# Channel attention taps read from PSUM, and five steps of a transformer pipeline in another order

## The chip, the cores and the metric

The kernel runs on one core of a Trainium2 chip. The metric is the device time of one execution in microseconds, the median of several runs. Engines are TensorE (PE; its weight loads are PEld), VectorE (DVE), ScalarE (ACT), GpSimd (POOL) and SyncE (SP, which issues all DMAs).

## The reference

A hybrid network over 16 images of 96 channels and 16x16 pixels, in four parts. Cut to what matters:

```python
x = x + conv_attention(group_norm(x))    # channel attention, 8 heads: q, k, v of 1x1 and depthwise 3x3 taps
x = large_conv_block(x)                  # 1x1, depthwise 13x13, gelu
t = tokens(x)                            # 16 x 256 tokens of 96
t = t + attention_2(ln(t))               # 6 heads over 512 tokens, own token masked
t = t + experts_2(ln(t))                 # 4 experts, top 2, hidden 384
t = t + attention_3(ln(t))               # causal
t = t + experts_3(ln(t))

# channel attention, per image (d = 12 channels a head, n = 256 pixels)
qkv = depthwise3x3(einsum('bchw,oc->bohw', x, w_qkv))
q, k = l2norm(q), l2norm(k)
attn = softmax(einsum('bhdn,bhen->bhde', q, k) * temperature)
out = einsum('bhde,bhen->bhdn', attn, v) @ w_proj
```

## The kernel before

The engines run programs of their own and meet at semaphores; the order on each engine is written out by hand. There are three stages.

**Channel attention** (`channel_attention`, 45 to 222 us) is a pipeline over 16 images; image b is worked on in `slot` b % 2. In step b TensorE computes the products of queries and keys of image b+1 (`queries_keys`) and its values with the nine value taps (`value_taps`, laid between the other work), and, for image c = b-1, turns q and scaled k (`turn`), multiplies the scores and applies the attention (`result`). ScalarE copies the raw products of queries and keys from PSUM bank 0 or 1 to the SBUF tile `raw` (`keep`, L449). VectorE applies the nine depthwise taps to them (`convolve`): L612 writes the first one, L615 adds the other eight, for q and k in turn, each as sum <- raw x tap + sum, 18 instructions an image. Seven taps stand before `maximum` of the image before, one between it and `attention`, the last behind. For image c ScalarE squares and sums q and k (`squares`), POOL makes the inverse norms out of the two sums (`norms`: L299, L301, L303, on 96x2 numbers), and ScalarE scales k by them (`scale_k`, L464). TensorE may overwrite a bank of raw products once ScalarE has copied it (`pe.wait_ge(s_raw, b)`).

**The large convolution** (222 to 323 us) is not touched.

**The transformer** (`transformer`, 324 us on) is a software pipeline over 16 pairs of images, i, the first 8 for layer 2 and the last 8 for layer 3, in two halves u each, one image a half (n = 2i + u). In half (i, u) run: attention of image n; the rest of attention of image n-1 (`weighted_values`, `turn_heads`, `turn_out`, `project`); two of the four experts (e0, e1) of pair j = i-2. In the first half (u = 0) also queries and keys of pair i+1, in the second (u = 1) values of i+1, the input of the experts of i-1 and the transposed input of i+2.

The scores of an image come in three blocks (`scores(n, 0..2)`) from which VectorE takes maxima; these are split in three bf16 parts, turned by TensorE (`turn_maxima`, L1087), copied by ScalarE as rows beside the queries (`rows`, L1288, `tr_qs`), and the scores are computed again, transposed, with the maxima subtracted (`transposed_scores(n, 0..2)`, L1095). ScalarE takes the exponential of each block (`exponential`, L1295, to `tr_pT`), and POOL sets the masked ones to zero (`masked(n, 0)` waits for the second exponential, `masked(n, 1)` for the third; L999). The third block uses the same PSUM banks as the first, so it waits for the first exponential; the next image's first scores (L1079) wait for the third one.

Queries and keys go into the products as three bf16 parts each: ScalarE makes the first from PSUM (`first_part`) and the second from VectorE's rest (`second_part`, L1284), POOL the third (`third_parts`, L993), and SP carries them through DRAM into the stacks `qs` and `ks` of the next pair. The experts' input is split too: `xh` (`high_input`, ScalarE, L1316) and `xl` (`low_input`, POOL, L988). The first product of an expert (`hidden`, L1143) needs both. `result` (L1153) is the second product: 24 matmuls in the trace for 4 blocks of tokens and 3 of hidden. `add_experts` (VectorE, L1492) adds it to the tokens, `add_bias` (L1500) adds the bias, `gates` (13 small instructions up to L1480) computes the gate. The two preloads of ScalarE's tables (L1333, L1345) stand at fixed places of a half.

## Time and profile before

| | us |
|---|---|
| median of 3 runs | 1042.7 (1040.33 to 1043.45) |
| the profiled execution | 1046.85 |
| its span | 1045.1 |

| stretch of the span, us | length | PE | DVE | ACT | POOL | TensorE clock |
|---|---|---|---|---|---|---|
| 60 to 180, channel attention | 120 | 94.7 | 73.2 | 47.7 | 36.1 | 0.79 |
| 180 to 255, its end and the start of the convolution | 75 | 54.6 | 41.8 | 23.0 | 38.2 | 0.68 |
| 300 to 1045, nearly all transformer | 745 | 633.9 | 399.8 | 427.5 | 313.1 | 0.92 |

The clock is the share of TensorE's full speed that was granted: 1.00 is 2.4 GHz and 0.50 is 1.2 GHz, and a mean between them mixes stretches at either. A busy TensorE is not one at its peak. The idle time in square brackets is what an engine spent before an instruction, with the engine, tile and line that ended it; times of instructions that overlap in the engine's pipeline are longer than their distance from start to start.

### The profile page before, as it was taken

How to read it: one execution, taken by the hardware profiler on the slowest of the kernel's cores; microseconds unless marked ns; L12 is line 12 of the kernel's file. 1: busy time of each engine (PE TensorE's matmuls, PEld its weight loads, DVE VectorE, ACT ScalarE, POOL GpSimd, SP SyncE). 2: the span in 40 equal slices, each digit the busy share in tenths (PEclk: the TensorE clock that was granted, in tenths of full speed). 3: DMA queues.
4: the chain of work that ended last, by engine and by line, in shares of the span. 5: the costliest groups of instructions: out<-in, count | busy, mean ns of one | idle time of the engine just before them, and what ended most of it. 6: DMA issues, size and time to landing. Idle time of an engine off the chain costs nothing.

```text
span 1045.1 us, 17189 instructions
## 1 busy us (share of the span) xinstructions
PE 857.4 (82%) x6224; PEld 697.2 (67%) x6224; DVE 576.9 (55%) x1684; ACT 515.6 (49%) x809; POOL 405.8 (39%) x428
## 2 busy tenths in 40 slices
PE   2878778678984375989998898998998998998887
PEld 1655556447983254777776786787787787777776
DVE  5855666628644236566557647656656555555431
ACT  1234334340013234566566676575575575575554
POOL 3232232346004124436436345355454444444422
PEclk9987877758996568799899999999999999999899
DMA  3700000001100333032030230230230330330000
GB/s 77 118 13 0 0 0 0 1 0 18 20 1 2 67 69 68 2 68 63 7 69 24 46 69 16 55 68 11 60 69 18 68 69 14 71 69 9 9 1 16
DMA packets 29000, 37.20 MB, mean 36 GB/s; under 512 B 10696, under 2 KB 25856, under 8 KB 28928
## 3 DMA queue, kind: packets, MB, share of 16 engines
q1 hardware_dynamic: 28928, 36.24, 16.6%
q8 instruction: 45, 0.74, 0.3%
q14 instruction: 27, 0.22, 0.1%
HBM read 25.06 MB, written 11.17 MB: 35 GB/s over the span
## 4 chain that ended last, share of the span: by engine, by line
PE 40%; ACT 11%; issue 6%; DVE 5%; POOL 5%; DMA 1%; SPq 1%; POOLq 0%; DVEq 0%; ACTq 0%
PE ps L1143 11%; PE ps L1153 9%; ACT tr_pT L1295 4%; PE ps L1079 4%; PE ps L1108 3%; PE ps L1095 3%; PE ps L1064 3%; POOL tr_pT L999 2%; ACT tr_hid L1311 2%; ACT tr_qs L1288 2%; PE ps L1081 2%; ACT L1345 2%; POOL tr_xl L988 2%; DVE tr_mf L1403 2%; PE ps L1113 1%
## 5 line engine op out<-in xcount | busy, mean ns | idle before, releaser
L1311 ACT ACTIVATE tr_hid<-ps,b 128x512 f32<-128x512 f32 x192 | 131.9, 688 | 136.4 <-PE ps L1143 135.8
L1153 PE MATMUL ps<-w,tr_hid 128*128 128x96 f32 x1536 | 182.4, 275 | 4.1 <-DVE tok L1492 4.1
L1153 PEld LDWEIGHTS ps<-w,tr_hid 128*128 128x128 f32 x1536 | 177.9, 192 | 6.4 <-issue 5.0
L999 POOL TENSOR_SCALAR_AFFINE_SELECT tr_pT<-tr_pT 128x768 f32<-128x768 f32 x64 | 55.4, 866 | 308.3 <-ACT tr_pT L1295 308.3
L1403 DVE TENSOR_REDUCE tr_mf<-ps 128x4 f32<-128x1024 f32 (+2 forms) x96 | 103.7, 1088 | 81.6 <-PE ps L1081 80.9
L1295 ACT ACTIVATE tr_pT<-ps 128x1024 f32<-128x1024 f32 (+1 forms) x96 | 86.3, 917 | 82.0 <-PE ps L1095 82.0
L1492 DVE SCALAR_TENSOR_TENSOR tok<-ps,tr_gate,tok 128x96 f32<-128x96 f32 x224 | 55.6, 311 | 121.6 <-PE ps L1153 119.6
L1079 PE MATMUL ps<-keys,tr_qs 96*128 96x256 bf16 (+1 forms) x384 | 77.7, 280 | 44.0 <-ACT tr_pT L1295 29.5
L1143 PE MATMUL ps<-tr_xh,tr_wh 96*128 96x512 f32 x192 | 90.1, 469 | 20.7 <-POOL tr_xl L988 19.5
L615 DVE SCALAR_TENSOR_TENSOR ca_qk<-ca_raw,dw,ca_qk 96x225 f32<-96x225 f32 (+1 forms) x256 | 98.8, 452 | 0.0
L299 POOL TENSOR_SCALAR ca_rn<-ca_ss 96x2 f32<-96x2 f32 x16 | 39.5, 2468 | 133.5 <-ACT ca_sq L455 133.5
L1079 PEld LDWEIGHTS ps<-keys,tr_qs 96*128 96x128 bf16 x384 | 39.7, 104 | 72.5 <-issue 43.6
L363 PE MATMUL ps<-ca_xn,wT 96*96 96x240 f32 (+2 forms) x288 | 85.6, 448 | 0.0
L1143 PE MATMUL ps<-tr_xh,tr_wl 96*128 96x512 f32 x192 | 78.8, 410 | 0.0
L1143 PE MATMUL ps<-tr_xl,tr_wh 96*128 96x512 f32 x192 | 78.1, 407 | 0.0
L363 PEld LDWEIGHTS ps<-ca_xn,wT 96*96 96x96 f32 x288 | 58.9, 210 | 18.0
L1143 PEld LDWEIGHTS ps<-tr_xh,tr_wh 96*128 96x128 f32 x192 | 37.3, 194 | 39.0 <-POOL tr_xl L988 22.6
L1288 ACT COPY tr_qs<-ps 18x1536 bf16<-18x1536 bf16 x32 | 45.8, 1432 | 31.9 <-PE ps L1087 31.6
L1095 PE MATMUL ps<-tr_qs,keys 114*128 114x256 bf16 (+1 forms) x384 | 51.6, 274 | 1.5 <-ACT tr_qs L1288 0.8
L1391 DVE TENSOR_TENSOR tr_rest<-ps,tr_part 96x512 f32<-96x512 f32 x32 | 22.0, 687 | 46.9 <-ACT tr_part L1280 46.9
L713 PE MATMUL ps<-cv_cin,cv_packed 128*128 x208 | 39.7, 354 | 6.6 <-DVE cv_packed L773 4.0
L993 POOL TENSOR_TENSOR tr_part<-tr_rest,tr_part 96x512 bf16<-96x512 f32 x32 | 42.2, 1336 | 5.9 <-ACT tr_part L1284 4.0
(234 smaller groups left out, 1731.2 us busy)
## 6 DMA issues: line engine op xcount, KB each, us to landing
parts<-tr_part SPq DMA_DIRECT2D x96, 96.0 KB
tr_qs<-parts SPq DMA_DIRECT2D x16, 288.0 KB, 4.2
keys<-parts SPq DMA_DIRECT2D x16, 288.0 KB, 5.4
tr_qs<-parts SPq DMA_DIRECT2D x16, 192.0 KB, 5.7
keys<-parts SPq DMA_DIRECT2D x16, 192.0 KB, 6.3
w<-in_L_ffn_w SPq DMA_DIRECT2D x4, 576.0 KB
chan<-in_x SPq DMA_DIRECT2D x4, 384.0 KB, 5.1
windows<-lines_d SPq DMA_DIRECT2D x96, 13.0 KB, 1.6
```

The lines of the kernel that those rows point to most:

```text
L363: ins = nc.tensor.matmul(dst[:, y0:y1, x0:x1], m.wT[0:C, M_V0 + 3 * (dy + 1) + dx + 1, :], x[:, y0 + dy:y1 + dy, x0 + dx:x1 + dx], start=( ...
L615: nc.vector.scalar_tensor_tensor(dst[:, y0:y1, x0:x1], src[:, y0 + dy:y1 + dy, x0 + dx:x1 + dx], m.dw0[:, t, k:k + 1], dst[:, y0:y1, x0:x1 ...
L999: pool.affine_select(out=block, in_=block, compare_op=ALU.is_ge if causal(n // 2) else ALU.not_equal, fill=0.0, base=0, pattern=[[0, H], [ ...
L1079: nc.tensor.matmul(view[:, c, :], qs[0:C, slot, h, u, P * t:P * (t + 1)], ks[0:C, slot, h, u, 0:width], start=True, stop=False)
L1095: ins = nc.tensor.matmul(view[:, c, :], ks[:, slot, h, u, P * t:P * (t + 1)], qs[:, slot, h, u, N - width:N], start=True, stop=True)
L1143: ins = nc.tensor.matmul(ps[:, H0 + step % 2, :], w[:, e, P * c:P * (c + 1)], x[:, :], start=(n == 0), stop=(n == 2))
L1153: ins = nc.tensor.matmul(ps[:, RES, C * t:C * (t + 1)], hid[:, e % 2, c, P * t:P * (t + 1)], m.ffn[j // PAIRS].w2[:, e * HC + c, :], start ...
L1288: nc.scalar.copy(qs[C:KR, n // 2 % 2, :, n % 2, :], max_rows()).then_inc(s_mr, 1)
L1295: nc.scalar.activation(flat[:, H * t + h:H * t + h + len(units), N - width:N], slot_view(slot_bank(k), len(units), width), ACT.Exp).then_i ...
L1311: nc.scalar.activation(hid[:, e % 2, c, :], ps[:, H0 + step % 2, :], ACT.Gelu, bias=m.ffn[j // PAIRS].b1[:, step:step + 1]).then_inc(s_h, 1)
L1403: nc.vector.tensor_reduce(mf[:, n % 2, 0, H * t + h:H * t + h + len(units)], slot_view(slot_bank(k), len(units), width), AX.X, ALU.max, ne ...
L1492: ins = nc.vector.scalar_tensor_tensor(fin[:, t, :] if last else m.tok[:, tile, :], ps[:, RES, C * t:C * (t + 1)], gate[:, tile, e:e + 1], ...
```

## The change

Channel attention: `keep`, the tile `raw` and its semaphore are gone. `convolve` reads the raw products from the PSUM bank. VectorE waits for TensorE's products directly, and TensorE waits for all nine taps of image b-1, for q and for k, before it writes the bank again.

Transformer, TensorE: `result` is cut in two parts of 12 matmuls each. `turn_maxima` stands between the parts of e0, and `transposed_scores(n, 2)` between the parts of e1, ahead of `project` and `gate_products`. ScalarE: `second_part` of both images stands behind the third exponential instead of before it. POOL: `low_input` stands before `masked(n, 1)` instead of behind it. `rows` stays on ScalarE.

```diff
@@ channel attention, TensorE
-                            pe.wait_ge(s_raw, b)
+                            for t in range(2):
+                                pe.wait_ge(s_tap[t], 9 * b)
                         queries_keys(b + 1, other)
@@ channel attention, ScalarE
-                def keep(b, slot):
-                    act.wait_ge(s_qk, b + 1)
-                    nc.scalar.copy(raw[:, slot, :, :].rearrange("p t n -> p (t n)"), ps[0:C, slot, :]).then_inc(s_raw, 1)
...
-                    if ahead:
-                        if back:
-                            for t in range(2):
-                                act.wait_ge(s_tap[t], 9 * b)
-                        keep(b + 1, other)
@@ channel attention, VectorE
-                            src = raw[:, slot, t, :].rearrange("p (y x) -> p y x", x=WW)
+                            src = ps[0:C, slot, N * t:N * (t + 1)].rearrange("p (y x) -> p y x", x=WW)
...
-                    dve.wait_ge(s_raw, b + 1)
+                    dve.wait_ge(s_qk, b + 1)
@@ transformer, POOL
+                        if u == 1 and 0 <= i - 1 < LAST:
+                            low_input(i - 1)
                         if i < LAST:
                             masked(n, 1)
-                        if u == 1 and 0 <= i - 1 < LAST:
-                            low_input(i - 1)
@@ transformer, TensorE
-                def result(j, e):
-                    pe.wait_ge(s_h, 12 * j + 3 * e + 3)
-                    if j or e:
-                        pe.wait_ge(s_ac, 4 * j + e)
-                    for t in range(4):
+                def result(j, e, part):
+                    if part == 0:
+                        pe.wait_ge(s_h, 12 * j + 3 * e + 3)
+                        if j or e:
+                            pe.wait_ge(s_ac, 4 * j + e)
+                    for t in range(2 * part, 2 * part + 2):
...
+                        result(j, e0, 0)
                     if att:
                         turn_maxima(n)
...
-                        result(j, e0)
+                        result(j, e0, 1)
...
-                        result(j, e1)
+                        result(j, e1, 0)
+                    if att:
+                        pe.wait_ge(s_ex, 3 * n + 1)
+                        transposed_scores(n, 2)
+                    if ffn:
+                        result(j, e1, 1)
                     if chain:
                         project(n - 1)
...
-                    if att:
-                        pe.wait_ge(s_ex, 3 * n + 1)
-                        transposed_scores(n, 2)
@@ transformer, ScalarE
                         first_part(i + 1, 1, H1)
-                        second_part(i + 1, 0)
-                        second_part(i + 1, 1)
...
                         exponential(n, 2)
+                    if u == 0 and i + 1 < LAST:
+                        second_part(i + 1, 0)
+                        second_part(i + 1, 1)
```

The rows below are instructions in program order, with the semaphores that they wait for.

TensorE, from the turned maxima to the next scores, in a second half with expert work. First before:

```order
L1087 MATMUL ps<-ident_b,maxima 114x128 [waits at_max_parts]
L1153 MATMUL ps<-w_2,tr_hid 128x96 [waits ff_added,ff_gelu]
L1095 MATMUL ps<-tr_qs,keys 128x256 [waits at_max_rows]
L1069 MATMUL ps<-wT,tr_xT 128x96 [waits at_rest1,ff_gelu]
L1153 MATMUL ps<-w_2,tr_hid 128x96 [waits ff_added,ff_gelu]
L1153 MATMUL ps<-w_2,tr_hid 128x96 x11
L1133 MATMUL ps<-wT,outT 128x96 [waits at_outT]
L1166 MATMUL ps<-gate,tr_xTF 128x4 [waits ff_xT,at_v_kept]
L1095 MATMUL ps<-tr_qs,keys 128x256 [waits at_exp]
L1058 MATMUL ps<-ident,tr_xnA 96x128 [waits at_normed,ff_xT]
L1079 MATMUL ps<-keys,tr_qs 128x256 [waits at_exp,at_stacks0]
```

And now:

```order
L1144 MATMUL ps<-w_2,tr_hid 128x96 [waits ff_added,ff_gelu]
L1144 MATMUL ps<-w_2,tr_hid 128x96 x5
L1077 MATMUL ps<-ident_b,maxima 114x128 [waits at_max_parts]
L1144 MATMUL ps<-w_2,tr_hid 128x96 x6
L1085 MATMUL ps<-tr_qs,keys 128x256 [waits at_max_rows]
L1059 MATMUL ps<-wT,tr_xT 128x96 [waits at_rest1,ff_gelu]
L1085 MATMUL ps<-tr_qs,keys 128x256 [waits at_exp]
L1144 MATMUL ps<-w_2,tr_hid 128x96 x6
L1123 MATMUL ps<-wT,outT 128x96 [waits at_outT]
L1158 MATMUL ps<-gate,tr_xTF 128x4 [waits ff_xT,at_v_kept]
L1048 MATMUL ps<-ident,tr_xnA 96x128 [waits at_normed,ff_xT]
L1069 MATMUL ps<-keys,tr_qs 128x256 [waits at_exp,at_stacks0]
```

The turned maxima have half a result ahead of them, and the third transposed scores (the second row that reads `tr_qs,keys`) have half a result, the projection and the gate products behind them.

POOL in the same half, around the experts' low input `tr_xl` and the masks on `tr_pT`. Before:

```order
L961 TENSOR_TENSOR tr_xnA<-tr_xnA,rstd 128x384 [waits at_pool_own]
L999 AFFINE_SELECT tr_pT<-tr_pT 128x6x128 [waits at_exp] x2
L988 TENSOR_TENSOR tr_xl<-tr_xTF,tr_xh 96x512 [waits ff_x_high]
L1010 TENSOR_TENSOR tr_bias<-tr_gate,b_2 128x384 [waits ff_tok_biased,ff_gate_dve]
L1010 TENSOR_TENSOR tr_term<-tr_gate,b_2 128x384 [waits ff_bias_own]
```

And now:

```order
L951 TENSOR_TENSOR tr_xnA<-tr_xnA,rstd 128x384 [waits at_pool_own]
L989 AFFINE_SELECT tr_pT<-tr_pT 128x6x128 [waits at_exp]
L978 TENSOR_TENSOR tr_xl<-tr_xTF,tr_xh 96x512 [waits ff_x_high]
L989 AFFINE_SELECT tr_pT<-tr_pT 128x6x128 [waits at_exp]
L1000 TENSOR_TENSOR tr_bias<-tr_gate,b_2 128x384 [waits ff_tok_biased,ff_gate_dve]
```

The low input stands between the two masks. ScalarE in a first half, from the first exponential on. Before:

```order
L1295 ACTIVATE tr_pT<-ps 128x1024 [waits at_scoresT]
L1280 CAST tr_part<-ps 96x2x256 [waits at_parts_stored,at_qk]
L1284 CAST tr_part<-tr_rest 96x2x256 [waits at_rest1] x2
L1295 ACTIVATE tr_pT<-ps 128x1024 [waits at_scoresT]
L1333 ACT_TABLE_LOAD
```

And now:

```order
L1291 ACTIVATE tr_pT<-ps 128x1024 [waits at_scoresT]
L1276 CAST tr_part<-ps 96x2x256 [waits at_parts_stored,at_qk]
L1291 ACTIVATE tr_pT<-ps 128x1024 [waits at_scoresT]
L1280 CAST tr_part<-tr_rest 96x2x256 [waits at_rest1] x2
L1329 ACT_TABLE_LOAD
```

The two second parts (`tr_part<-tr_rest`) have moved behind the last exponential of the half.

## Rows read from the trace of the kernel before

**Rows 1.** Windows between maxima: length, busy PE, PEld, DVE, ACT, POOL, clock

```profile
81.09:93.11 12.02, 11.70 (x40) 8.42 (x40) 7.25 (x23) 4.77 (x15) 2.51 (x3) 0.58 0.00 0
...
117.37:128.21 10.84, 7.84 (x40) 5.71 (x40) 7.23 (x22) 4.50 (x14) 3.73 (x3) 0.95 0.00 0
...
sum 155.08, PE 119.28 PEld 88.05 DVE 94.06 ACT 60.55 POOL 46.75; mean PE 9.18 PEld 6.77 DVE 7.24 ACT 4.66 POOL 3.60
```

**Rows 2.** DVE timeline: start us, us, instruction, [idle before <-releaser]

```profile
119.61 0.60 DVE L612 TENSOR_SCALAR ca_qk<-ca_raw,dw 96x256 f32<-96x256 f32 x2
120.14 4.54 DVE L615 SCALAR_TENSOR_TENSOR ca_qk<-ca_raw,dw,ca_qk 96x225 f32<-96x225 f32 x12
128.21 0.25 DVE L621 TENSOR_REDUCE ca_nm<-ps 96x1 f32<-96x96 f32 x1 [3.54 <-PE ps L405]
```

**Rows 3.** Timelines of POOL and ScalarE around the norms, and the last image

```profile
120.67 0.42 ACT L455 ACTIVATE ca_sq<-ca_qk 96x256 f32<-96x256 f32 x1 [0.26 <-DVE ca_qk L615]
...
121.92 2.83 POOL L299 TENSOR_SCALAR ca_rn<-ca_ss 96x2 f32<-96x2 f32 x1 [8.03 <-ACT ca_sq L455]
124.84 0.71 POOL L301 TENSOR_TENSOR ca_rn<-ca_rn,power 96x2 f32<-96x2 f32 x1
...
125.84 0.51 ACT L464 ACTIVATE ca_kn<-ca_qk,ca_rn 96x256 f32<-96x256 f32 x1 [3.59 <-POOL ca_rn L303]
...
216.81 0.21 POOL L299 TENSOR_SCALAR ca_rn<-ca_ss 96x2 f32<-96x2 f32 x1 [6.88 <-ACT ca_sq L455]
217.10 0.71 POOL L301 TENSOR_TENSOR ca_rn<-ca_rn,power 96x2 f32<-96x2 f32 x1
```

**Rows 4.** Line L299: ns least/median/most, first and last start us

```profile
L299 POOL TENSOR_SCALAR ca_rn<-ca_ss x16: 214/2505/3763, 40.4 to 216.8; 96x2 f32<-96x2 f32 x16
```

**Rows 5.** L993 on POOL (ns min/median/max, starts), DVE timeline beside it

```profile
L993 POOL TENSOR_TENSOR tr_part<-tr_rest,tr_part x2: 1151/1378/1606, 608.3 to 609.8; 96x512 bf16<-96x512 f32 x2
...
608.30 0.55 DVE L1500 TENSOR_TENSOR tok<-tok,tr_bias 128x384 f32<-128x384 f32 x1
608.88 0.99 DVE L1492 SCALAR_TENSOR_TENSOR tok<-ps,tr_gate,tok 128x96 f32<-128x96 f32 x4
```

**Rows 6.** Timeline of TensorE in a step at full clock

```profile
126.40 0.38 PE L395 MATMUL ps<-ident,ca_qk 96*128 96x96 f32 x2 [2.67 <-ACT ca_kn L464]
...
132.09 1.76 PE L363 MATMUL ps<-ca_xn,wT 96*96 96x256 f32 x8
137.25 0.58 PE L395 MATMUL ps<-ident,ca_qk 96*128 96x96 f32 x2 [3.40 <-ACT ca_kn L464]
```

**Rows 7.** Windows of 2 us, columns as in Rows 1

```profile
100.00:102.00 2.00, 0.00 (x0) 0.00 (x0) 0.41 (x2) 0.42 (x2) 1.38 (x3) 0.84 0.00 0
102.00:104.00 2.00, 1.86 (x7) 1.55 (x8) 0.00 (x0) 1.48 (x4) 0.00 (x0) 0.50 0.00 0
```

**Rows 8.** TensorE waits from 300 us on: us in total, times, longest

```profile
PE ps L1079 <- ACT tr_pT L1295: 29.5, 31, 3.1
PE ps L1143 <- POOL tr_xl L988: 19.5, 15, 3.1
PE ps L1087 <- DVE maxima L1417: 16.7, 12, 5.6
```

**Rows 9.** Timelines of ScalarE, TensorE, VectorE in one pair of halves

```profile
588.23 1.02 ACT L1295 ACTIVATE tr_pT<-ps 128x1024 f32<-128x1024 f32 x1 [3.26 <-PE ps L1095]
...
591.46 0.50 PE L1143 MATMUL ps<-tr_xh,tr_wh 96*128 96x512 f32 x1 [1.23 <-POOL tr_xl L988]
...
594.29 2.36 DVE L1403 TENSOR_REDUCE tr_mf<-ps 128x4 f32<-128x1024 f32 x2
...
595.98 0.28 PE L1079 MATMUL ps<-keys,tr_qs 96*128 96x256 bf16 x1
...
600.18 0.32 PE L1087 MATMUL ps<-ident_b,maxima 128*114 128x128 bf16 x2 [0.86 <-DVE maxima L1417]
...
610.69 0.28 PE L1079 MATMUL ps<-keys,tr_qs 96*128 96x256 bf16 x1 [1.12 <-ACT tr_pT L1295]
```

More of the change, by code:

```diff
@@ L177, in channel_attention @@
     s_tap = [sem(f"ca_tap{t}") for t in range(2)]
-    (s_xn, s_qk, s_raw, s_v, s_vc, s_ss, s_rn, s_kn, s_T, s_trs, s_sc, s_mx, s_nm, s_ex, s_rc, s_at, s_ap, s_aps, s_out, s_x1) = (
-        sem(f"ca_{n}") for n in ("normed", "qk", "qk_kept", "v", "v_kept", "squares", "norms", "k_scaled", "turned", "turned_kept",
+    (s_xn, s_qk, s_v, s_vc, s_ss, s_rn, s_kn, s_T, s_trs, s_sc, s_mx, s_nm, s_ex, s_rc, s_at, s_ap, s_aps, s_out, s_x1) = (
+        sem(f"ca_{n}") for n in ("normed", "qk", "v", "v_kept", "squares", "norms", "k_scaled", "turned", "turned_kept",
                                  "scores", "max", "shift", "exp", "recip", "attn", "attnproj", "attnproj_kept", "out", "x1"))
@@ L190, in channel_attention @@
         xn = sb("ca_xn", [C, 2, N])
-        raw = sb("ca_raw", [C, 2, 2, N])
         qkc = sb("ca_qk", [C, 2, 2, N])
@@ L520, in _ @@
                 normed(1, 1)
-                keep(0, 0)
                 steps(act, step)
@@ L1154, in result @@
                                                    m.ffn[j // PAIRS].w2[:, e * HC + c, :], start=(c == 0), stop=(c == HC - 1))
-                    ins.then_inc(s_Y, 1)
+                    if part == 1:
+                        ins.then_inc(s_Y, 1)
                 def turn_experts(j, bank):
@@ L1215, in half @@
                         hidden(j, e1, 2)
+                    if ffn:
+                        if u == 0 and PAIRS <= i - 3:
+                            pe.wait_ge(s_oc, i - 3 - PAIRS + 1)
+                        result(j, e0, 0)
                     if att:
@@ L1218, in half @@
                     if ffn:
-                        if u == 0 and PAIRS <= i - 3:
-                            pe.wait_ge(s_oc, i - 3 - PAIRS + 1)
-                        result(j, e0)
+                        result(j, e0, 1)
                     if chain:
@@ L1245, in half @@
                     if ffn:
-                        result(j, e1)
+                        result(j, e1, 0)
+                    if att:
+                        pe.wait_ge(s_ex, 3 * n + 1)
+                        transposed_scores(n, 2)
+                    if ffn:
+                        result(j, e1, 1)
                     if chain:
```

## The prediction

> **What bounds the kernel now.** I read the stages first, then the one repeated step of each stage that the change touches, then the wait that ends last in it. Two stretches matter: the pipeline of channel attention (16 images, 45 to 221 us of the span) and the transformer's pipeline (from 324 us on).
>
> In channel attention the step of one image repeats every 155.08 / 13 = 11.93 us (the edges of the stretches in [rows 1] are the starts of VectorE's `maximum`). VectorE is not its limit: from the maximum at 117.37 us to the end of the next image's first taps, at 120.14 + 4.54 = 124.68 us, it needs 7.31 us, and then it sits idle for 3.54 us until the scores come [rows 2]. The scores wait for a chain: squares (ScalarE), norms (POOL), scaled keys (ScalarE), transposes and scores (TensorE). In that chain one row is odd. POOL's L299, a maximum over 96x2 numbers, takes 2.83 us and ends at 124.75 us, 0.07 us after VectorE's last tap; for the last image, when VectorE runs no tap, it takes 0.21 us [rows 3]. Its median over 16 images is 2.5 us, its least 0.21 us [rows 4]. It does not work for 2.5 us; it is held until VectorE's taps stop. From start to start the hold is there too: L301 follows L299 after 2.92 us in the middle and after 0.29 us at the end [rows 3]. The Trainium skill (Perfetto Trace Analysis, on the GPSIMD Engine Instruction) calls a GPSIMD instruction's reported span unreliable; by that rule L299's length alone would prove nothing and part 1 could gain nothing, and the spacing it asks for instead agrees with the length here.
>
> What in the taps holds POOL? Today each tap (L615) reads two operands from SBUF, the copied products `ca_raw` and the sum `ca_qk`. A later stretch shows both kinds beside a POOL instruction: of two equal POOL subtractions (L993) the first took 1606 ns and the second 1151. The first began at 608.26 us and ran beside VectorE's L1500, both of whose inputs are in SBUF, for 0.55 us, and is 0.46 us longer; then beside four L1492, whose inputs are one PSUM and one SBUF tile, and these added nothing [rows 5]. So it is two SBUF operands that hold POOL, and L1492 has just the form that the taps get by this change.
>
> The hold costs twice. While POOL is held TensorE has nothing to do (3.40 us in [rows 6]), and behind such a gap the granted clock falls: it is 0.84 in a stretch with TensorE idle and 0.50, the 1.2 GHz level, right after it [rows 7]. The step from 81.09 us ran at a mean clock of 0.58 with TensorE busy for 11.70 of 12.02 us; the one from 117.37 us, at 0.95, needed 7.84 busy us [rows 1].
>
> **Part 1, the taps read PSUM.** It removes 16 copies from ScalarE (they lie between the scaled keys and the turned ones, while ScalarE waits for TensorE's transposes, and are worth nothing by themselves) and the two-SBUF form of 256 taps. It adds one wait: TensorE's `queries_keys(b+1)` now waits for all taps of image b-1, and the value taps and transposes queue behind it. Those taps end about 2.3 us after a maximum, while TensorE comes to that line some 3 us after it at full clock (before the value taps at 132.09 us, 3.9 us after the maximum at 128.21 us [rows 2, 6]), so it is covered by 0.7 us.
>
> Three limits remain for a step, all at full clock:
> - The chain. Squares to scaled keys took 125.84 - 120.67 = 5.17 us [rows 3]; without the hold (2.92 - 0.29 = 2.63 us) it is 2.54 us. Then 0.56 us to TensorE's transposes, 128.21 - 126.40 = 1.81 us from there to the next maximum [rows 2, 6]; and squares can start some 2.6 us after a maximum, when the last tap is out (the next image's L612 started 2.24 us after one [rows 2]). Sum 7.5 us.
> - TensorE, from the transposes at 126.40 us to the end of the value taps at 132.09 + 1.76 us: 7.45 us [rows 6].
> - VectorE, 7.31 us and what PSUM costs it. Twelve taps in 4.54 us are 0.37 us from start to start for 232 elements on average; four L1492 in 0.99 us are 0.23 us for 96 [rows 2, 5]. The line through both is 1.06 ns an element and 0.13 us fixed, which leaves nothing for PSUM. Only the two L612, 0.26 us apart now, would go to a tap's pace, 0.13 us more each: 7.6 us.
>
> I take 7.8 us, the largest with 0.2 us for what they do to each other. TensorE's gap is then under half a microsecond, so the clock should stay at full speed. There are 14 such steps (the 13 of [rows 1] and one like them before): 14 x (11.93 - 7.8) = 58 us. Bounds: 63 us at TensorE's 7.45 us; and 44 us if a tap holds up the next until its end, which by L1492's own 0.31 us and 136 elements more would be 0.45 us a tap, 18 x 0.08 us more, a step of 8.8 us.
>
> The Trainium skill speaks against this edit (VectorE: DVE Perf Modes, "The TRN2 errata"): it gives a fixed cost of 58 cycles with an SBUF source and 120 with a PSUM source at 0.96 GHz, which would be, as an estimate from that page, 65 ns more for each of 18 taps and about the same 14 us less gain. The line through the two rows does not show this difference.
>
> **Part 2, the transformer's order.** TensorE's idle time there has three repeated causes [rows 8]: the next scores wait for the third exponential (29.5 us), the experts' first product waits for POOL's `low_input` (19.5 us), the turned maxima wait for VectorE (16.7 us). [Rows 9] show one pair of halves.
> - The third transposed scores move ahead of half of an expert's `result`, of `project` and the gate products. ScalarE sat idle for 3.26 us before that exponential; it now runs 2 to 2.6 us earlier. Nearly all waits for it go: 26 of 29.5 us; the first pairs, which have no expert work, keep some.
> - `low_input` no longer stands behind the second `masked`, which itself waited for that exponential. Its input has been ready for microseconds, so it is done before TensorE comes: 19.5 less the longest, 3.1, which is the last pair, where nothing moves: 16.4 us.
> - The maxima's transposes get half a `result` in front of them; the wait of 0.86 us goes, also in the other pairs with expert work: 5 us. The large ones, up to 5.6 us, are in pairs 0 and 1 and stay.
>
> These 47 us are counted from the end of the instruction before; in a stream matmuls overlap (1.76 us for eight value taps [rows 6]), which I put at 0.15 us each, so 53 waits less are 8 us more: 55 us.
>
> Against that, what is late next. VectorE gets no earlier: its gates end at 594.29 us, where its first maximum starts; half a microsecond earlier at most, as its copy L1447 no longer meets `low_input`. TensorE comes to the third scores, which need that maximum, 2 us before 595.98 us, and waits about 0.9 us in 9 pairs (in 5 pairs the turned outputs lie between). On POOL the second `masked` stands behind `third_parts`, and these behind ScalarE's second parts, which the change puts behind the third exponential: weighted values wait some 0.5 us. The rows copy, and the copy of the next input, are reached 0.5 us early in all. That is 1.9 us in 9 pairs and 1.0 in 5, an estimate of 22 us. Net 33 us, and 2 us for halves that ran at the lower clock behind two waits in a row: 35 us. Bounds: 17 us if each new wait is twice that, 45 if half.
>
> **Sum.** 58 + 35 = 93 us. The profiled execution took 1046.85 us (its span is 1045.1), 4.15 us over the median of the runs, 1042.7: 950 us.
>
> **Rivals.**
> - Dearer taps (0.45 us each, VectorE the bound at 8.8 us): 44 + 35, 963 us. For: VectorE is the nearest bound anyway. Against: L1492's pace.
> - The new order of the transformer yields only half, since the waits reappear behind VectorE's long queue of gates and maxima: 58 + 17, 968 us.
> - Part 1 brings nothing, since POOL stays held by a tap's one SBUF read, or since the clock stays low and TensorE needs its 12 us: 35 us alone, 1008 us. Against: rows 5, and that the gaps ahead of each fall are gone.
> - Slower. VectorE reads each tap from a bank beside those that TensorE writes. If a tap then cost over 0.76 us from start to start instead of 0.37, its step would be over 14.3 us, and 14 x 2.4 us eat the 35 us of part 2; at 0.85 us a step is 16 us and the kernel takes 1065 us. Nothing shows it: L1492 reads PSUM while TensorE writes other banks.
>
> **How the numbers follow.** Forecast 0.70 (935 to 967 us), dearer taps 0.08, half the second part 0.08, part 1 without effect 0.08, slower 0.03, and 0.03 for under 935 us. The range 930 to 980 us takes in the first three and the bounds (62.7 + 45 and a few microseconds of clock below, 44 + 17 above). A difference of 0.3% is about what a measurement of this kernel can tell from none: faster by more 0.96, within it 0.01, slower by more 0.03.
>
> **What would show it.** L299 at 0.2 us in all steps; maxima every 7.6 to 8 us from 46 us on; the clock at 1.00 from there to 200 us; the taps 0.37 us apart; the transformer's start 55 to 60 us earlier; no wait of TensorE for `tr_xl` but the last; a new wait of the third scores (bf16, L1069 of the changed kernel) for the maximum of VectorE. I am wrong if L299 still ends with VectorE's taps, or if taps are 0.44 us apart or more.

## The result, and the profile after

The changed kernel takes 920.3 us (median of 4 runs, 919.64 to 924.86), against 1042.7 us before: a ratio of 0.884, with a 95% interval of 0.881 to 0.887. It is 122.4 us faster. Forecast were 950 us, with a range of 930 to 980: the time lies 30 us under the forecast and 10 us under the range.

The profiled execution after has a span of 918.0 us (919.73 us in all) against 1045.1. The 127.1 us of difference lie here (each stretch ends at the first maximum of the next):

| stretch | before | after | less |
|---|---|---|---|
| up to channel attention's first maximum | 45.67 | 44.36 | 1.3 |
| channel attention, first to last maximum | 175.55 | 112.59 | 63.0 |
| last maximum to the transformer's first | 134.33 | 132.61 | 1.7 |
| transformer, from its first maximum to the end | 689.55 | 628.44 | 61.1 |

**Channel attention.** Two steps of the changed kernel, as in [rows 1] (length; busy TensorE, weight loads, VectorE, ScalarE, POOL; granted clock):

```profile
96.57:103.99 7.42, 7.10 (x41) 5.49 (x41) 7.35 (x22) 4.33 (x14) 1.10 (x3) 1.00 0.00 0
103.99:111.50 7.51, 7.18 (x40) 5.19 (x39) 7.43 (x24) 4.16 (x14) 1.10 (x3) 1.00 0.00 0
```

The 14 steps of 11.96 us on average became 14 of 7.46, 13 of them at a clock of 1.00 and the last, where TensorE has less to do, at 0.88. (Behind it the clock is as low as before: 0.50 in the last image's 8.1 us.) Of each VectorE is busy for all but 0.07 or 0.08 us: it is the bound now, with TensorE close behind it. POOL's maximum over 96x2 (before in [rows 4]), its place in a step and VectorE's taps (before in [rows 2, 3]):

```profile
L298 POOL TENSOR_SCALAR ca_rn<-ca_ss x16: 210/212/234, 38.5 to 152.5; 96x2 f32<-96x2 f32 x16
...
100.20 0.21 POOL L298 TENSOR_SCALAR ca_rn<-ca_ss 96x2 f32<-96x2 f32 x1 [6.04 <-ACT ca_sq L451]
...
99.59 4.48 DVE L605 SCALAR_TENSOR_TENSOR ca_qk<-ps,dw,ca_qk 96x225 f32<-96x225 f32 x12
```

The maximum takes 0.21 us in every step, in the middle of VectorE's taps. Twelve taps take 4.48 us from PSUM; from SBUF they took 4.54.

**Transformer.** TensorE's waits from 250 us on (us in all, times, longest), before in [rows 8]:

```profile
PE ps L1077 <- DVE maxima L1414: 10.9, 4, 5.5
PE ps L1098 <- issue: 4.3, 10, 2.2
...
PE ps L1069 <- DVE tr_mf L1400: 4.1, 8, 0.6
PE ps L1133 <- DVE tr_xT L1382: 3.8, 13, 0.3
PE ps L1098 <- POOL tr_pT L989: 2.2, 1, 2.2
PE ps L1069 <- ACT tr_pT L1291: 1.9, 2, 1.1
```

The next image's scores' wait for the third exponential fell from 29.5 to 1.9 us, the experts' wait for `tr_xl` from 19.5 to nothing, the maxima's from 16.7 to 10.9. Against that stand waits that weren't there. One pair of halves, as in [rows 9], from TensorE, POOL and VectorE:

```profile
506.11 3.48 DVE L1400 TENSOR_REDUCE tr_mf<-ps 128x4 f32<-128x1024 f32 x3
...
507.39 0.28 PE L1069 MATMUL ps<-keys,tr_qs 96*128 96x256 bf16 x1 [0.52 <-DVE tr_mf L1400]
...
519.69 0.28 PE L1069 MATMUL ps<-keys,tr_qs 96*128 96x256 bf16 x1
...
521.98 0.86 POOL L989 TENSOR_SCALAR_AFFINE_SELECT tr_pT<-tr_pT 128x768 f32<-128x768 f32 x1
...
522.94 1.07 PE L1098 MATMUL ps<-tr_pT,values 128*32 128x256 f32 x16 [0.29 <-issue]
...
539.80 0.47 PE L1133 MATMUL ps<-tr_xh,tr_wh 96*128 96x512 f32 x1 [0.30 <-DVE tr_xT L1382]
```

The third scores of a first half wait 0.52 us for the first maximum, as was foreseen. The weighted values wait 0.29 us, and POOL's second `masked`, which ends at 522.84, is what they wait for though the view says "issue". The pair takes 37.55 us instead of 40.84.

The whole stretch in one window each, the changed kernel first and the kernel before under it:

```profile
289.56:918.00 628.44, 586.80 (x5088) 494.23 (x5086) 370.57 (x1155) 412.32 (x548) 292.07 (x331) 0.97 0.21 46
```

```profile
355.55:1045.10 689.55, 611.19 (x5088) 500.04 (x5086) 379.88 (x1155) 413.57 (x548) 297.83 (x331) 0.94 0.19 42
```

The same 5088 matmuls were busy for 24.4 us less, and TensorE was idle for 41.6 us instead of 78.4, 36.7 us less. The sum is the 61.1 us. The prediction had 35.

### The profile page after: what moved, and what is told of

Its sections match the earlier page's. It is cut to its first block, busy times and chain, and to the rows that moved or that the text cites. A ratio compares the mean times of both kernels' runs of the same rounds, so it can differ in the third digit from the quotient of the medians.

```text
span 918.0 us, 17153 instructions
## 1 busy us (share of the span) xinstructions
PE 799.0 (87%) x6224; PEld 666.3 (73%) x6224; DVE 569.6 (62%) x1684; ACT 505.6 (55%) x793; POOL 363.4 (40%) x428
## 4 chain that ended last, share of the span: by engine, by line
PE 52%; ACT 8%; DVE 8%; issue 2%; POOL 1%; DMA 1%; SPq 1%; DVEq 0%; POOLq 0%
PE ps L1144 14%; PE ps L1133 12%; PE ps L1085 5%; PE ps L1069 4%; PE ps L1054 4%; ACT tr_hid L1307 3%; PE ps L1098 3%; ACT tr_qs L1284 3%; ACT L1341 2%; PE ps L1071 2%; DVE tr_mf L1400 2%; PE ps L1059 2%; PE ps L1123 1%; PE ps L1158 1%; PE ps L1111 1%
## 5 line engine op out<-in xcount | busy, mean ns | idle before, releaser
L1144 PE MATMUL ps<-w,tr_hid 128*128 128x96 f32 x1536 | 189.4, 275 | 4.1 <-DVE tok L1489 4.1
L1144 PEld LDWEIGHTS ps<-w,tr_hid 128*128 128x128 f32 x1536 | 184.5, 192 | 8.9 <-issue 4.9
L605 DVE SCALAR_TENSOR_TENSOR ca_qk<-ps,dw,ca_qk 96x225 f32<-96x225 f32 (+1 forms) x256 | 97.7, 446 | 0.0
L1133 PE MATMUL ps<-tr_xh,tr_wh 96*128 96x512 f32 x192 | 87.0, 453 | 5.5 <-DVE tr_xT L1382 3.8
L1069 PE MATMUL ps<-keys,tr_qs 96*128 96x256 bf16 (+1 forms) x384 | 73.3, 269 | 20.9 <-DMA keys<-parts 14.9
L362 PE MATMUL ps<-ca_xn,wT 96*96 96x240 f32 (+2 forms) x288 | 67.1, 373 | 0.0
L362 PEld LDWEIGHTS ps<-ca_xn,wT 96*96 96x96 f32 x288 | 47.2, 168 | 11.3
L1000 POOL TENSOR_TENSOR tr_bias<-tr_gate,b 128x384 f32<-128x384 f32 x16 | 13.3, 834 | 83.8 <-DVE tr_gate L1477 83.8
L983 POOL TENSOR_TENSOR tr_part<-tr_rest,tr_part 96x512 bf16<-96x512 f32 x32 | 36.5, 1160 | 23.8 <-ACT tr_part L1280 23.8
L1085 PEld LDWEIGHTS ps<-tr_qs,keys 114*128 114x128 bf16 x384 | 35.4, 104 | 14.4 <-ACT tr_qs L1284 6.9
```

Of the source, the lines that this page charges most:

```text
L362: ins = nc.tensor.matmul(dst[:, y0:y1, x0:x1], m.wT[0:C, M_V0 + 3 * (dy + 1) + dx + 1, :], x[:, y0 + dy:y1 + dy, x0 + dx:x1 + dx], start=( ...
L605: nc.vector.scalar_tensor_tensor(dst[:, y0:y1, x0:x1], src[:, y0 + dy:y1 + dy, x0 + dx:x1 + dx], m.dw0[:, t, k:k + 1], dst[:, y0:y1, x0:x1 ...
L1069: nc.tensor.matmul(view[:, c, :], qs[0:C, slot, h, u, P * t:P * (t + 1)], ks[0:C, slot, h, u, 0:width], start=True, stop=False)
L1085: ins = nc.tensor.matmul(view[:, c, :], ks[:, slot, h, u, P * t:P * (t + 1)], qs[:, slot, h, u, N - width:N], start=True, stop=True)
L1133: ins = nc.tensor.matmul(ps[:, H0 + step % 2, :], w[:, e, P * c:P * (c + 1)], x[:, :], start=(n == 0), stop=(n == 2))
L1144: ins = nc.tensor.matmul(ps[:, RES, C * t:C * (t + 1)], hid[:, e % 2, c, P * t:P * (t + 1)], m.ffn[j // PAIRS].w2[:, e * HC + c, :], start ...
```

## Experiments

All were timed beside runs of the kernel before on the same chip, whose medians lie between 1041.5 and 1042.2 us. "Stretch" is the profiled time from the transformer's first maximum to the end: 689.6 us before, 628.4 after, 628.9 in a second profile of the changed kernel.

### Each part alone

The first is part 1, every hunk of the diff above the transformer; the second is part 2, every hunk in it.

> The kernel before with part 1 alone (taps from PSUM), the transformer in its old order. Theory (the parts are independent; the transformer gained 60.7 us by itself): only the 66.4 us go by which the transformer started earlier, so 1042.7 - 66.4 = 976 us, with the step of channel attention at 7.46 us, and the transformer's pairs at 40.84 us and its clock between 0.96 and 1.00 as before. Rival (part of the transformer's gain came from a clock history that part 1 left behind): the transformer gets shorter here too, by up to 20 us, 956 to 970 us.

Measured: 982.8 us (981.66 to 985.85), ratio 0.945 (0.940 to 0.950), 59.3 us less than before. The stretch:

```profile
291.25:980.80 689.55, 611.29 (x5088) 500.12 (x5086) 379.73 (x1155) 413.15 (x548) 297.47 (x331) 0.94 0.19 42
```

689.55 us, to the hundredth what it was. Part 1 leaves nothing behind in the transformer, and the rival is out. The time is 7 us above the expected 976. The span is 64.3 us shorter. The expectation took 66.4 us for the earlier start of the transformer (by the two profiles it is 66.0), and took it off the median, while it came from a profiled run that lay 4.15 us above it.

> The kernel before with part 2 alone (third transposed scores, low input, turned maxima and second parts moved). Theory (new order alone removes the waits, and with them the falls of the clock): 1042.7 - 60.7 = 982 us, pairs of 37.5 us, clock 1.00 in nearly all of them. Rival (the 35 us of the prediction were right and the rest is part 1's doing): 1007 us, with pairs whose clock stays at 0.96 to 0.98.

Measured: 982.6 us (981.46 to 984.27), ratio 0.945 (0.940 to 0.949), 59.4 us less. The stretch:

```profile
351.24:979.80 628.56, 586.77 (x5088) 494.15 (x5086) 371.04 (x1155) 412.55 (x548) 292.46 (x331) 0.97 0.21 46
```

The new order gives its 61 us by itself. 59.3 + 59.4 = 118.7 of the 122.4 us: the parts add up within 4 us.

### Part 1: the hold and the clock

```diff
 def turn(c, slot):
-    pe.wait_ge(s_kn, c + 1)
     pe.wait_ge(s_trs, c + 1)
+    for k in range(8):
+        nc.tensor.matmul(ps[0:C, 4, 0:2 * C]..., m.wT[0:C, M_V0, :], m.wT[0:C, M_V0:M_V0 + 2, :], start=True, stop=True)
+    pe.wait_ge(s_kn, c + 1)
```

> The kernel before, with 8 idle-time products of TensorE (96x192, result never read) issued while it waits for the scaled keys in channel attention; taps and POOL as before. It separates the hold of POOL from the clock. Theory (most of the step's 4.4 us is the hold, and the clock adds what the steps at 0.6 to 0.8 cost): L299 stays near 2.5 us, the clock stays near 1.00, and the step becomes that of the steps that ran at full clock before, 10.84 us, so 14 x 1.1 = 15 us less, about 1027 us. Rival (the clock is the larger part, and with it at full the step comes near 7.5 us): about 980 us.

Measured: 1034.3 us (1029.29 to 1035.78), ratio 0.992 (0.989 to 0.994), 8 us less. A step, and in it POOL's maximum:

```profile
102.02:112.87 10.85, 9.72 (x56) 8.02 (x56) 7.24 (x23) 4.67 (x15) 4.66 (x3) 1.00 0.00 0
...
105.64 3.77 POOL L299 TENSOR_SCALAR ca_rn<-ca_ss 96x2 f32<-96x2 f32 x1 [6.03 <-ACT ca_sq L458]
```

```profile
L299 POOL TENSOR_SCALAR ca_rn<-ca_ss x16: 214/3640/3772, 39.9 to 204.1; 96x2 f32<-96x2 f32 x16
```

With TensorE never idle for long the clock is 1.00 and 13 steps take 10.82 to 10.86 us, the forecast of the first theory. So of the 4.5 us of a step 1.1 are the clock and 3.4 the hold. The hold itself did not stay near 2.5 us, as the theory had it: its median is 3.6 us. The maximum still ends with VectorE's last tap.

Why 8 us came out and not 15: between the two profiles the stage is 12.3 us shorter, 14.9 in 14 steps less 2.6 in the last one, which the filler made 10.74 us long instead of 8.15. The rest is the run that it is compared with. The profiled run before has long steps, 11.96 us on average; in the profiles of e2, e11 and e12, where this stage is the same, they take 11.74 to 11.80 us, so that the clock is worth 0.8 to 1.1 us a step.

```diff
-src = raw[:, slot, t, :].rearrange("p (y x) -> p y x", x=WW)
+src = (ps[0:C, slot, N:2 * N] if t else raw[:, slot, 0, :]).rearrange("p (y x) -> p y x", x=WW)
```

> The kernel before, with the keys' taps (every second tap) reading PSUM and the queries' taps still reading the copy in SBUF. Theory (each tap with two SBUF operands holds POOL only while it runs, and POOL gets in at the next tap that reads PSUM): POOL's maximum over 96x2 lasts at most 0.7 us, the step is 7.5 to 7.9 us, and the time about 1042.7 - 60 = 982 us. Rival (POOL stays locked out as long as any tap with two SBUF operands is queued): it still ends with VectorE's last tap, 2 to 3 us, and the time stays at 1035 to 1043 us.

Measured: 987.0 us (983.84 to 991.62), ratio 0.950 (0.945 to 0.955). VectorE's taps come from SBUF and PSUM in turn, and POOL's maximum stands between them:

```profile
86.88 0.44 DVE L616 SCALAR_TENSOR_TENSOR ca_qk<-ps,dw,ca_qk 96x225 f32<-96x225 f32 x1
87.24 0.46 DVE L616 SCALAR_TENSOR_TENSOR ca_qk<-ca_raw,dw,ca_qk 96x240 f32<-96x240 f32 x1
87.61 0.46 DVE L616 SCALAR_TENSOR_TENSOR ca_qk<-ps,dw,ca_qk 96x240 f32<-96x240 f32 x1
...
87.23 0.53 POOL L299 TENSOR_SCALAR ca_rn<-ca_ss 96x2 f32<-96x2 f32 x1 [6.02 <-ACT ca_sq L456]
```

```profile
L299 POOL TENSOR_SCALAR ca_rn<-ca_ss x16: 212/408/537, 39.5 to 156.2; 96x2 f32<-96x2 f32 x16
```

The maximum comes with the tap that reads `ca_raw`, and ends 0.15 us into the next tap, which reads PSUM. It never takes more than 0.54 us, and most steps are 7.6 us. So a tap with two SBUF operands holds POOL while it runs and no longer; what made 0.21 us into 1.6 to 3.8 us in the steps before was that the next such tap stood right behind it, every time. Half the taps in PSUM are nearly as good as all (982.8 us in e1), and ScalarE's copy, which this run keeps, was not what cost the time. The Trainium skill says that a VectorE instruction with two SBUF inputs and a GpSimd one lock each other out "for the whole instruction" (SBUF — State Buffer, "SBUF: two separate sides"). This trace agrees, with 0.54 us at most, and adds that between such instructions in a row POOL got no turn.

The two taps also settle the rival of dearer taps: 0.44 us each and 0.36 from start to start at 225 elements, 0.46 and 0.38 at 240, from SBUF or PSUM alike. The 65 ns more for each tap that the prediction drew as an estimate from the Trainium skill (VectorE: DVE Perf Modes, "The TRN2 errata") are not there.

### Part 2: which of the moves

Four kernels, e5 to e8, each take one move back out of the changed kernel.

```diff
 if ffn:
     result(j, e1, 0)
-if att:
-    pe.wait_ge(s_ex, 3 * n + 1)
-    transposed_scores(n, 2)
 if ffn:
     result(j, e1, 1)
...
     gate_products(i - 1, H1)
+if att:
+    pe.wait_ge(s_ex, 3 * n + 1)
+    transposed_scores(n, 2)
```

> The changed kernel with only the third transposed scores put back behind result, project and the gate products. Theory (of part 2's 61 us, 36.7 are idle time and 24.4 are the same products at a higher clock, and the waits for the third exponential also make the clock fall): 30 us of waits come back, less what they hide elsewhere, and the clock falls to 0.96 to 0.98 in part of the pairs: 920 + 30 + 10 = 950 to 965 us. Rival (the sum of the prediction: 26 us of waits and next to no clock): 940 to 947 us with the clock at 1.00.

Measured: 953.6 us (951.81 to 955.48), 33 us above the changed kernel. Its waits:

```profile
PE ps L1069 <- ACT tr_pT L1290: 25.8, 31, 1.1
...
PE ps L1098 <- issue: 13.0, 14, 2.2
```

From the fourth pair to the last but one the clock stays at 1.00, where the theory had 0.96 to 0.98, and what comes back there is waiting (39.3 us a pair, 37.7 causal). But in the first three pairs, and from the last pair on, it is lower than in the changed kernel (0.50, 0.72, 0.97 and 0.95 against 0.61, 0.85, 1.00 and 0.98); the second, the third and the last:

```profile
322.09:360.20 38.11, 27.64 (x195) 20.85 (x194) 22.48 (x51) 14.73 (x20) 14.75 (x14) 0.72 0.22 47
360.20:402.79 42.59, 39.88 (x361) 32.68 (x363) 25.27 (x78) 27.12 (x36) 17.75 (x20) 0.97 0.20 43
...
862.38:952.30 89.92, 78.28 (x597) 65.97 (x595) 34.05 (x127) 50.16 (x67) 30.79 (x35) 0.95 0.04 10
```

Of the 34 us of the stretch that come back, 22 are idle time of TensorE and 12 are busy time. The idle time is 24 us for the exponential and 9 for the weighted values behind POOL's late `masked`, less what the waits for VectorE lose. Of the busy time some 10.5 us lie in the first three pairs and from the last pair on. So the theory's two terms are both there, the clock's in other pairs than it said.

```diff
-if u == 1 and 0 <= i - 1 < LAST:
-    low_input(i - 1)
 if i < LAST:
     masked(n, 1)
+if u == 1 and 0 <= i - 1 < LAST:
+    low_input(i - 1)
```

> The changed kernel with only low_input put back behind the second masked on POOL. Theory (with the third scores early, the second masked no longer waits, so this move was worth nothing by itself): within 2 us of 920. Rival (the prediction's separate term of 16.4 us for this move): 930 to 937 us, with TensorE waiting for tr_xl in some 14 pairs.

Measured: 921.8 us (921.15 to 923.44), at most 1.4 us above the changed kernel; pairs of 37.55 us. The move is worth next to nothing once the third scores are early.

```diff
-result(j, e0, 0)
 if att:
     turn_maxima(n)
 if ffn:
+    result(j, e0, 0)
     result(j, e0, 1)
```

> The changed kernel with the turned maxima back in front of the whole result of the first expert. Theory (VectorE's maxima are done at 511.24 us in the pair looked at, when TensorE gets there at 510.56 us; in the other half of the pair both come together): 0.7 to 0.9 us a pair, 10 to 13 us, 930 to 933 us. Rival (the prediction's term): 5 us, 925 us.

Measured: 927.3 us (926.98 to 928.41), 7 us above: pairs of 38.36 us (0.8 more), causal ones of 36.06 (0.3 more). Between theory and rival; the prediction's 5 us were near.

```diff
     first_part(i + 1, 1, H1)
+    second_part(i + 1, 0)
+    second_part(i + 1, 1)
...
     exponential(n, 2)
-if u == 0 and i + 1 < LAST:
-    second_part(i + 1, 0)
-    second_part(i + 1, 1)
```

> The changed kernel with the second parts back in front of the third exponential on ScalarE. Theory (the exponential then ends some 1.3 us later in every first half, and TensorE's next scores, the masked block and the weighted values wait for it): 0.6 to 1 us in 14 pairs, 928 to 934 us. Rival (TensorE has enough other work before it needs the exponential): 918 to 922 us.

Measured: 920.2 us (918.05 to 924.34), the same as the changed kernel. The non-causal pairs are 0.3 us longer (37.85), the causal ones 0.1 shorter (35.64). The rival was right.

Two kernels put one move each into the kernel before. The first:

```diff
-if i < LAST:
-    masked(n, 1)
 if u == 1 and 0 <= i - 1 < LAST:
     low_input(i - 1)
+if i < LAST:
+    masked(n, 1)
```

> The kernel before with only low_input moved ahead of the second masked. It asks what this move is worth where the third scores are late. Theory (the two moves take away the same delay, the one that the late third exponential causes, so each alone gets what the other would): 16 to 22 us less than before, 1020 to 1026 us, though undoing the same move in the changed kernel cost 1.4 us. Rival (the move is worth little anywhere, and the experts' first product then waits for something else): 1037 to 1042 us.

Measured: 1012.0 us (1004.37 to 1014.68), ratio 0.969 (0.965 to 0.973), 30 us less than before. The waits for `tr_xl` are gone, those for the exponential stay:

```profile
PE ps L1079 <- ACT tr_pT L1295: 30.2, 31, 3.3
...
354.60:1011.10 656.50, 596.26 (x5088) 491.61 (x5086) 364.00 (x1155) 412.55 (x548) 297.47 (x331) 0.96 0.20 44
```

The second has the other side of e6's and e7's diffs: part 2 as in e2, with `low_input` and `turn_maxima` where they were. ScalarE's second parts, worth nothing by e8, have moved in it too.

> The kernel before with only the third transposed scores and the second parts moved; low_input and the turned maxima stay. Theory (this move also brings the second masked and low_input forward; of the 59.4 us of the whole part 2 only the 7.4 us of the maxima and the 1.4 us of low_input are missing): 989 to 993 us, no wait for tr_xl in the pairs in the middle. Rival (the prediction's terms, 26 us and their clock, stand apart from the 16.4 us of low_input): 1005 to 1015 us, and waits for tr_xl remain.

Measured: 990.5 us (988.34 to 992.77), ratio 0.950 (0.948 to 0.953), 51.4 us less. Of the 19.5 us of waits for `tr_xl` one of 0.8 us is left, although `low_input` still stands behind `masked`:

```profile
PE ps L1143 <- POOL tr_xl L988: 0.8, 1, 0.8
```

So `low_input` alone gives 30 us in the old order and 1.4 in the new one; the third scores alone give 51 us. 30 + 51 is more than the 59.4 us of both with the maxima: the two moves remove one delay, that of the late third exponential, in two places.

### The clock of the transformer, its order unchanged

In the kernel before, the granted clock falls in some pairs. One such place, windows of 2 us and TensorE's waits in them:

```profile
866.00:868.00 2.00, 1.06 (x14) 0.71 (x12) 1.65 (x5) 1.98 (x3) 1.32 (x2) 1.00 0.01 4
868.00:870.00 2.00, 1.17 (x4) 0.98 (x5) 1.83 (x6) 0.02 (x1) 0.77 (x1) 0.84 0.00 0
870.00:872.00 2.00, 2.00 (x9) 1.49 (x8) 1.74 (x6) 1.33 (x2) 0.92 (x2) 0.50 0.00 0
...
866.76 0.22 PE L1079 MATMUL ps<-keys,tr_qs 96*128 96x128 bf16 x1 [0.55 <-ACT tr_pT L1295]
868.83 0.50 PE L1143 MATMUL ps<-tr_xh,tr_wh 96*128 96x512 f32 x1 [1.21 <-POOL tr_xl L988]
```

Two waits, 0.55 and 1.21 us long, that end 2.1 us apart, and then the 1.2 GHz level. But the same two waits one pair earlier have no fall behind them:

```profile
827.93 0.22 PE L1079 MATMUL ps<-keys,tr_qs 96*128 96x128 bf16 x1 [0.55 <-ACT tr_pT L1295]
829.99 0.50 PE L1143 MATMUL ps<-tr_xh,tr_wh 96*128 96x512 f32 x1 [1.21 <-POOL tr_xl L988]
...
830.00:832.00 2.00, 2.00 (x11) 1.67 (x12) 1.69 (x10) 1.00 (x2) 0.00 (x0) 1.00 0.04 8
```

At the end of 13 pairs, the third to the fifteenth, a wait of 1.2 us for `tr_xl` stands behind one of 0.55 to 0.99 us for the exponential, and the clock falls behind 5 of these 13. What decides which, no run shows. The experiment fills the second wait:

```diff
-    pe.wait_ge(s_xl, j + 1)
     pe.wait_ge(s_wl, j // PAIRS + 1)
     pe.wait_ge(s_xT, min(i + 2, LAST))
     pe.wait_ge(s_nm, j + 1)
+    for k in range(3):
+        nc.tensor.matmul(ps[0:C, H0, 0:2 * C]..., m.wT[0:C, M_V0, :], m.wT[0:C, M_V0:M_V0 + 2, :], start=True, stop=True)
+    pe.wait_ge(s_xl, j + 1)
```

> The kernel before in its old order, with 3 products of TensorE (96x192, result never read) in front of its wait for the low input, once a pair; the wait itself stays. Theory (the clock falls in the pairs where a wait of 0.5 to 0.9 us for the third exponential is followed within 2 us by this one of 1.2 us, and the falls are a loss of their own): all pairs from the fourth on at a clock of 1.00, the pairs in the middle still 40.84 us, the causal ones 38.6 instead of 38.6 to 40.1, some 10 to 18 us less than before, 1024 to 1032 us. Rival (the low clock is absorbed by the waits it shortens, so all of the 61 us come from the waits): 1039 to 1044 us although the clock is at 1.00.

Measured: 1036.9 us (1031.31 to 1039.79), ratio 0.994 (0.992 to 0.996). A pair in the middle and a causal one:

```profile
551.86:592.70 40.84, 37.84 (x336) 31.36 (x332) 25.40 (x78) 26.31 (x34) 19.40 (x22) 1.00 0.20 44
...
867.20:906.01 38.81, 36.71 (x326) 30.90 (x325) 22.60 (x69) 25.50 (x36) 18.23 (x20) 1.00 0.24 52
```

The lengths are as the theory had them: 40.84 us where the clock had been full, and 38.81 us for the causal pair that had taken 40.08 at a clock of 0.98. But the sum is 5 to 6 us, not 10 to 18: the stretch is 683.9 us, 5.7 less. One early pair became 1.8 us longer (44.36), and pairs whose clock had been 0.96 and 0.97 were as long as before (40.82 against 40.85, 38.61 against 38.63): there the low clock was hidden behind something else, probably VectorE's queue, which no run tested. With the second wait filled, to 0.2 us at most, no fall is left between the fourth pair and the last.

### Faster versions

```diff
 if u == 1 and 0 <= i - 1 < LAST:
     low_input(i - 1)
 if i < LAST:
     masked(n, 1)
+if u == 0 and i + 1 < LAST:
+    third_parts(i + 1)
```

(with `third_parts` gone from its place ahead of them)

> The changed kernel with the second masked ahead of third_parts on POOL, a try for a faster version. Theory (TensorE's weighted values wait 0.3 us in 10 first halves for a masked that stands behind third_parts; the parts' transfer has slack): 3 to 5 us less than 920. Rival (the parts leave POOL 0.9 us later and something in their chain, the sums of L1388 or the transfer, was just in time): 919 to 923 us.

Measured: 917.2 us (914.13 to 917.76), ratio 0.880 (0.878 to 0.881). The pairs are 37.2 us (0.35 less) and causal 35.5 (0.2 less), the waits for the weighted values are gone, and a wait of 2 us for the stacked keys has come at the start. 3 us less by the medians. The ratios' intervals touch, but each of its five runs (917.8 us at most) is below each of the changed kernel's (919.5 at least, with those of e15 below).

On top of e9's edit:

```diff
     first_part(i + 1, 1, H1)
+    if causal(i):
+        second_part(i + 1, 0)
+        second_part(i + 1, 1)
...
-if u == 0 and i + 1 < LAST:
+if u == 0 and i + 1 < LAST and not causal(i):
```

> e9_masked_first with, in the causal half of the pairs alone, the second parts back in front of the third exponential, where e8 had pairs of 35.64 us against 35.73. Theory (the two edits add up): 0.7 us less than e9, 912 to 917 us. Rival (masked first already took what the place of the second parts gives): the same as e9, causal pairs of 35.5 us.

Measured: 919.6 us (912.77 to 921.13); its causal pairs are 35.63 us, 0.13 longer than e9's, where the theory had them shorter. No gain; the edits don't add up.

> The changed kernel as it is, on the chip of e14_mixed_second_parts, so that the two can be compared. Theory: 919 to 921 us, 4 to 6 us above e14. Rival (the 3 us between e9 and the changed kernel were a difference of chips): within 1 us of e14.

Measured: 920.6 us (919.51 to 921.38), on the same chip. The changed kernel repeats within 0.3 us; e14 is 0.9 us below it, which is within what its own runs scatter. Part of that scatter is the clock at the end of the kernel: from the last pair's first maximum on, e14's profiled run, its fastest, takes 86.0 us at a clock of 1.00, the changed kernel's 87.6 at 0.98, and e8's, its slowest, 90.2 at 0.93.

In the changed kernel, before TensorE's two long waits at the transformer's start:

```diff
 pe.wait_ge(s_ones, 1)
+warm(38)
 turn_attention(0, H0)
...
 pe.wait_ge(s_r1, 2)
+pe.wait_ge(s_vp, 1)
+warm(36)
```

> The changed kernel with 38 and 36 products of TensorE (96x192, result never read) issued in its two long waits at the transformer's start (14.5 us for the first normed tokens, 14.9 us for the first stacked keys). Theory (the low clock behind these waits, 0.50 and 0.61 up to 321 us, costs what TensorE's 31 busy us there would shrink by, as far as they are on the path): 8 to 14 us less than 920, 906 to 912 us. Rival (the first pair waits for maxima, exponentials and turned rows, and a faster TensorE only waits longer, so that its clock falls again): 917 to 921 us.

Measured: 924.2 us (923.13 to 930.41), 4 us slower:

```profile
257.84 15.53 PE L1047 MATMUL ps<-wT 96*96 96x192 f32 x76 [6.65 <-POOL tr_xTF L1008]
```

The filler could begin only at 257.84 us, ran at the low clock at first, and held TensorE until 273.2 us, 8 us longer than its wait would have lasted (265.08 us in the changed kernel). The first maximum came 4.6 us later. That says nothing on the clock, so it was done again with 17 and 44 products on top of e9:

> e9_masked_first with 17 and 44 products of TensorE (96x192, result never read) in the two long waits at the transformer's start, where e10_warm_start had 38 and 36; 38 of them took 15.5 us after the start of the filler, and 7.2 us were free. Theory (the low clock at the start is on the path): first maximum 2 to 3 us after e9's distance from the end of channel attention shortens by as much, first pair 1.5 to 3 us shorter, 910 to 914 us. Rival (the start is bound by POOL, the stacks' transfer and VectorE): within 2 us of e9, 915 to 919 us, with the clock high all the same.

Measured: 913.6 us (912.77 to 915.41), ratio 0.877 (0.874 to 0.881). This is the fastest version: each of its 6 runs is below each of the 9 of the changed kernel, and its median is 6.7 us below the 920.3. How much of that the filler gives is not shown. From channel attention's last maximum to the transformer's first it takes 129.8 us against e9's 132.3; the first pair was 0.2 us shorter, and the second, whose clock was 0.69, 2.6 us longer than e9's. So at the end of the third pair nothing of the gain was left. The profiled run is 1.9 us shorter than e9's all the same (911.1 against 913.0), but 0.9 of that lies ahead of channel attention's first maximum and 1.5 in the end of the kernel, both of which scatter as much without the edit. The runs of the two (912.8 to 915.4 and 914.1 to 917.8) overlap.

## Why the prediction was wrong

The direction, the mechanism of part 1 and both places of part 2 were right. What failed is the sum of part 2: of its 26 us the largest share is a term for the clock, put at 2 us, where some 18 us of TensorE's busy time went. Four terms were off in all, and they add up: 5.0 + 3.0 + 26.1 - 4.15 = 30 us.

- **The step of channel attention, 7.8 us: it is 7.46.** The three limits were computed as 7.5, 7.45 and 7.6 us, and then 0.2 us put on top "for what they do to each other". VectorE, whose 7.6 us were the bound, is busy for 7.35 to 7.43 us and waits for nothing. 14 x 0.34 = 4.8 of the 63.0 - 58 = 5.0 us. The rest of part 1 held: no hold, full clock in 13 steps (not up to 200 us, as was said), taps 0.36 to 0.38 us apart, the two L602 at 0.86 us for both.
- **3.0 us ahead of and behind that stage** (1.3 + 1.7) were in no term. The runs spread as far there, whatever their kernel: the first maximum comes at 44.0 us in e1 and at 47.7 in e11, and the stretch behind the stage takes 134.3 us in e1 and 132.1 in e4. So I put the 3.0 us down to scatter. With them the transformer starts 66.0 us earlier, where 55 to 60 were expected.
- **Part 2, 35 us: it is 61.1.** Three slips. (a) The waits that go were put at 47 us and are 52.9 (27.6, 19.5 and 5.8 in the three lines): I took the longest wait for `tr_xl`, 3.1 us, for that of a last pair "where nothing moves". It belongs to the last pair but one, whose `low_input` did stand behind a `masked`:

```profile
983.60 0.86 POOL L999 TENSOR_SCALAR_AFFINE_SELECT tr_pT<-tr_pT 128x768 f32<-128x768 f32 x1 [3.03 <-ACT tr_pT L1295]
984.43 1.26 POOL L988 TENSOR_TENSOR tr_xl<-tr_xTF,tr_xh 96x512 fp32r<-96x512 f32 x1
...
985.75 0.80 PE L1143 MATMUL ps<-tr_xh,tr_wh 96*128 96x512 f32 x1 [3.06 <-POOL tr_xl L988]
...
986.00:988.00 2.00, 2.00 (x5) 1.57 (x6) 1.57 (x9) 0.57 (x1) 0.08 (x1) 0.50 0.00 0
```

  and behind it TensorE ran at 1.2 GHz. From the last pair's first maximum to the end the kernel before takes 95.2 us, the changed one 87.6 and e11, with this move alone, 87.9. (b) The new waits were put at 22 us and are 52.9 - 36.7 = 16.2. They are the ones named, but 0.52 us for the first maximum where I had 0.9, and 0.29 for `masked` where I had 0.5. (c) Busy time falls by 24.4 us where I had 10 (8 of overlap and 2 of clock). In the pairs at full clock it falls by 0.4 us each (36.83 to 36.40), some 6 us in 13 pairs, which is the overlap. The rest, some 18 us, is the clock, in the second pair (0.71 to 0.85, 5.8 us shorter), the third and fifth, in the causal pairs and from the last pair on. I had looked at a pair with a clock of 1.00 and taken it for all. e13 shows what the falls behind `low_input` cost as the order stood, 5.7 us; how much of the other 12 is a gain of its own and how much follows from shorter waits no run separates. Beside these, the bounds given for part 2 do not follow from its terms: with the new waits doubled it is 13 us and with half of them 46, where 17 and 45 were written.
- **The 4.15 us.** I took them off the sum to pass from the profiled run to the median. But the profiled run was long, in part at least, because its steps of channel attention were, in which the term of 58 us had already counted them. With the old stage they average 11.74 to 12.04 us in five profiles (before, e2, e11, e12, e13), which is 4 us in all, while the transformer takes 689.5 us in e1 as before. The changed kernel, whose steps do not vary, has its profiled run within 0.6 us of its median. This error went the other way and hid part of the rest.

The rivals: dearer taps are out by 0.36 to 0.38 us from start to start in either form (e4); part 1 without effect by e1; half of part 2 by e2. That the taps are not dearer was in part luck: the prediction drew a line through one row from SBUF and one from PSUM, and a line fits any two points, whatever PSUM costs. "Slower" needed taps over 0.76 us apart. The 3 in 100 below 935 us were too few: every bound in the sum was taken towards the slow side, and the range followed them.

That `low_input` was a term of 16.4 us beside the 26 us of the third scores was no slip of the sum, since each wait was counted once, but it would have misled anyone who took the terms for the worth of the edits: by e6 and e11 it is 1.4 or 30 us, as the third scores stand.

## What to carry to other kernels

When a short POOL instruction lasts as long as VectorE's row of instructions beside it, look at what these read: one operand from PSUM, even in every second of them, gave POOL its turn. When two waits stem from one late event, try each edit alone and with the other; the sum of the waits in the trace is not the worth of each edit. And before multiplying one repetition by their number, read the clock and the length of all of them: here the one looked at had a full clock and the others had not.
